# A DLRM tower on one core: the group loop written out, ten tables looked up by matmul, ids in small loads

## The reference

```python
e = jnp.stack([tbl_f[ids[:, f]] for f in range(27)], axis=1)      # 2048 x 27 x 128
z = jnp.einsum('bfd,bgd->bfg', e, e)[:, tril_i, tril_j]           # 2048 x 351
h = jnp.concatenate([z, dense_ctx], axis=1)                       # 2048 x 367
h = jnp.maximum(h @ W_top1 + b_top1, 0.0)                         # 512
h = jnp.maximum(h @ W_top2 + b_top2, 0.0)                         # 256
y = h @ W_top3                                                    # 1
```

## Time and profile before

| what | value |
| --- | --- |
| runs | 441.11, 441.77, 443.19 us |
| the profiled execution | 439.78 us, of it 437.9 us span |
| PE, matmul | 338.7 us busy, 77% |
| POOL | 297.9 us, 68% |
| DVE | 231.5 us, 53% |
| ACT | 212.2 us, 48% |
| mean granted clock of TensorE | 0.934 of full |
| bytes moved by DMA | 37.40 MB, mean 85 GB/s |
| table 0 landed, first lookup on PE | 19.92 us, 24.53 us |

### The profile page before, as it was taken

The page is one execution under the profiler, slowest core; times in us unless marked ns, Lnnn a source line. Parts: engine busy times, 40 slices in busy tenths (PEclk is TensorE's granted clock), DMA queues, the critical chain, the costliest instruction groups (busy, mean ns, idle before and its releaser), DMA issues.

```text
span 437.9 us, 14262 instructions
## 1 busy us (share of the span) xinstructions
PE 338.7 (77%) x5982; PEld 303.4 (69%) x5982; DVE 231.5 (53%) x907; ACT 212.2 (48%) x431; POOL 297.9 (68%) x308
## 2 busy tenths in 40 slices
PE   0071784798969898998843799799989789899778
PEld 0061683698859776987733798598869777897665
DVE  0290995497248623965431482487439544860430
ACT  1121746536573538434830136834584268436832
POOL 6777687777777777777777506777777777777020
PEclk9997798699998989999966599989999999999999
DMA  3748415265224522372227401236226922221000
GB/s 73 254 153 269 183 36 161 63 82 133 53 59 82 141 53 56 72 136 65 57 70 82 126 0 45 57 78 139 58 54 71 145 62 58 54 64 52 8 9 4
DMA packets 23740, 37.40 MB, mean 85 GB/s; under 512 B 6616, under 2 KB 17440, under 8 KB 23680
## 3 DMA queue, kind: packets, MB, share of 16 engines
q0 software_dynamic: 9600, 19.33, 15.7%
q10 hardware_dynamic: 10416, 10.75, 15.6%
q1 hardware_dynamic: 3664, 6.43, 4.2%
HBM read 35.61 MB, written 0.01 MB: 81 GB/s over the span
## 4 chain that ended last, share of the span: by engine, by line
PE 48%; SPq 12%; ACT 12%; DMA 11%; issue 11%; DVE 4%; ACTq 0%; DVEq 0%
SPq L280 12%; PE fill_ps L431 11%; PE fill_ps L433 10%; ACT et L544 9%; PE pair_ps L492 9%; PE mlp_ps L443 9%; PE mlp_ps L469 7%; DMA hot_ids<-ids_hot_d 4%; DMA work<-tbl_d 4%; DMA work<-dense_d 2%; DVE work L329 2%; DMA work<-work 1%; ACT work L329 1%; PE fill_ps L457 1%; DVE one_hot L638 1%
## 5 line engine op out<-in xcount | busy, mean ns | idle before, releaser
L394 POOL DMA_INDIRECT rows<-tbl_d,index x222 | 215.9, 973 | 82.3 <-issue 67.0
L431 PE MATMUL fill_ps<-one_hot,table_hi 128*128 128x256 f32 x610 | 159.6, 299 | 54.0 <-DVE table_lo L616 24.5
L431 PEld LDWEIGHTS fill_ps<-one_hot,table_hi 128*128 128x128 f32 x610 | 125.4, 206 | 56.4 <-issue 43.3
L433 PE MATMUL fill_ps<-one_hot,table_lo 128*128 128x256 f32 x610 | 157.1, 295 | 0.0
L638 DVE TENSOR_SCALAR one_hot<-hot_ids 128x256 fp32r<-128x256 f32 x610 | 137.3, 301 | 26.2 <-PE fill_ps L433 25.3
L329 DVE COPY work<-pair_ps 26x112 f32<-26x112 f32 (+1 forms) x256 | 66.0, 258 | 117.8 <-PE pair_ps L492 114.7
L433 PEld LDWEIGHTS fill_ps<-one_hot,table_lo 128*128 128x128 f32 x610 | 125.5, 206 | 0.0
L394 POOL DMA_INDIRECT rows<-tbl_d,ids_sb x72 | 78.1, 1084 | 26.4 <-issue 21.3
L552 ACT COPY et<-fill_ps 128x512 f32<-128x512 f32 (+1 forms) x37 | 42.5, 1148 | 106.5 <-PE fill_ps L433 102.6
L544 ACT COPY et<-fill_ps 128x512 f32<-128x512 f32 (+2 forms) x80 | 78.9, 1183 | 3.0 <-PE fill_ps L417 2.9
L492 PE MATMUL pair_ps<-et 128*26 128x26 f32 x4096 | 55.3, 196 | 29.9 <-issue 16.1
(11 more groups left out here) (24 smaller groups left out, 63.3 us busy)
## 6 DMA issues: line engine op xcount, KB each, us to landing
hot_ids<-ids_hot_d ACTq DMA_DIRECT2D x8, 1152.0 KB
rows<-tbl_d,index POOLq DMA_INDIRECT x222
work<-tbl_d SPq DMA_DIRECT2D x4, 512.0 KB, 18.5
work<-tbl_d SPq DMA_DIRECT2D x3, 640.0 KB, 16.4
rows<-tbl_d,ids_sb POOLq DMA_INDIRECT x72
w_sb<-w_d ACTq DMA_DIRECT2D x1, 768.0 KB, 4.8
w_sb<-tbl_d SPq DMA_DIRECT2D x1, 640.0 KB, 17.3
w_sb<-tbl_d SPq DMA_DIRECT2D x1, 512.0 KB, 17.9
```

The lines of the kernel that those rows point to most:

```text
L394: nc.gpsimd.indirect_dma_start(out=rows[:, t, c, :], out_offset=None, in_=tables[f], in_offset=bass.IndirectOffsetOnAxis(ap=numbers[:, f:f ...
L431: nc.tensor.matmul(to, table_hi[0:HOT_ROWS, CHUNK_AT[k] + c, :], hot, start=(c == 0), stop=False)
L433: last = nc.tensor.matmul(to, table_lo[0:HOT_ROWS, CHUNK_AT[k] + c, :], hot, start=False, stop=(c == HOT_CHUNKS[k] - 1))
```

## The change

The loop is gone; all groups are written out, and all engines walk one list of steps. In it the last two pair banks of a group stand between the lookups of the next one, and layer 2 is cut in two, so that no two pair banks touch but the last two. All groups use ten hot tables (90 chunks) and 17 cold ones. The hot ids come two tables at a time (256 KB), six loads ahead: the first six from ACT's queue, the others from SP's. They are no longer made local: DVE compares the raw int32 ids with a scalar per partition (`chunk_row`, the number of the row that the partition holds in this chunk). The one-hots lie in a ring of 20 chunks and are handed over by half tables. POOL and PE wait for each fill of up to four tables instead of each tile. ACT moves hot fills 0 and 1 only after it has moved bank 3 of the group before, since `et` is read until then. At the start, the long load of the other ids stands behind the first three tables.

```diff
-N_HOT = 9
-EARLY_HOT = (9, 9)
-LATE_HOT = (8, 9)
-HOT_RING = 3
+N_HOT = [10] * 8
+FILL_RING = 4
+IDS_RING = 6
+ONE_HOT_RING = 20
...
+def hot_fills(g):
+    return [(k, min(2, N_HOT[g] - k)) for k in range(0, N_HOT[g], 2)]
+def cold_fills(g):
+    n = FEATURES - N_HOT[g]
+    return [(c, min(4, n - c)) for c in range(0, n, 4)]
+def order():
+    steps = []
+    for g in range(GROUPS):
+        hot = [("hot", g, j) for j in range(len(hot_fills(g)))]
+        cold = [[("cold", g, t, j) for j in range(len(cold_fills(g)))] for t in range(GROUP_TILES)]
+        if g == 0:
+            steps += hot[:3] + cold[0] + hot[3:] + [("pairs", g, 0)] + cold[1][:2] + [("pairs", g, 1)] + cold[1][2:]
+        else:
+            b = g - 1
+            steps += [hot[0], ("pairs", b, 2), hot[1], ("pairs", b, 3), hot[2]] + cold[0][:2] + [hot[3]] + cold[0][2:4]
+            steps += hot[4:] + cold[0][4:] + [("layer1", b), ("pairs", g, 0)] + cold[1][:2]
+            steps += [("layer2", b, 0), ("pairs", g, 1)] + cold[1][2:] + [("layer2", b, 1), ("layer3", b)]
+    return steps + [("pairs", GROUPS - 1, 2), ("pairs", GROUPS - 1, 3)]
+STEPS = order()
...
+def halves(k):
+    n = CHUNKS_OF[k]
+    return (0, n // 2), (n // 2, n)
+def parts_in_the_way(end):
+    return sum(1 for last in ([0] + PART_ENDS)[:-1] if last < end - ONE_HOT_RING)
...
-        index = sb("index", [P, 2, GROUP_TILES * FEATURES], I32)
-        hot_ids = sb("hot_ids", [P, 2, N_HOT, COLS], I32)
-        one_hot = sb("one_hot", [P, HOT_RING, MAX_CHUNKS, COLS], F32R)
+        hot_ids = sb("hot_ids", [P, IDS_RING, 2 * COLS], I32)
+        one_hot = sb("one_hot", [P, ONE_HOT_RING, COLS], F32R)
...
-        def periods(engine, period, peeled=1):
-            period(0, 0)
-            period(0, 1)
-            with engine.Fori(1, GROUPS // 2 - peeled) as turn:
-                period(turn, 0)
-                period(turn, 1)
...
+        def load_hot_ids(engine, step):
+            _, g, j = step
+            k0, n = hot_fills(g)[j]
+            slot = HOT_FILL[step] % IDS_RING
+            engine.dma_start(hot_ids[:, slot, 0:n * COLS],
+                             ids_hot[g, k0 * COLS:(k0 + n) * COLS].partition_broadcast(P)
+                             ).then_inc(hot_ids_in[slot], 16)
...
         @block.sync
+            sp.dma_start(ids_sb[:, 0:FEATURES], ids[:, 0:FEATURES]).then_inc(first_ids_in, 16)
+            for k in range(3):
+                load_table(k)
+            sp.dma_start(ids_sb[:, FEATURES:], ids[:, FEATURES:]).then_inc(ids_in, 16)
+            for k in range(3, MOST_HOT):
+                load_table(k)
+            fills = list(HOT_FILL)
+            for step in STEPS:
+                if step[0] == "hot" and HOT_FILL[step] + IDS_RING < len(fills):
+                    sp.wait_ge(hot_made, parts_through(step))
+                    load_hot_ids(sp, fills[HOT_FILL[step] + IDS_RING])
+                elif step[0] == "pairs" and step[2] == PAIR_BANKS - 1 and step[1] < LAST:
+                    complete_zt(sp, step[1], ALL_LOWS, z_in)
+                elif step[0] == "layer3":
+                    store(step[1])
...
         @block.gpsimd
+                    for j, (c0, n) in enumerate(cold_fills(g)):
+                        if g > 0:
+                            freed = ("cold", g - 1, t, min(j, len(cold_fills(g - 1)) - 1))
+                            pool.wait_ge(cold_full, COLD_FILL[freed] + 1)
+                        for c in range(c0, c0 + n):
+                            f = COLD[c]
+                            nc.gpsimd.indirect_dma_start(
+                                out=rows[:, t, c, :], out_offset=None, in_=tables[f],
+                                in_offset=bass.IndirectOffsetOnAxis(
+                                    ap=ids_sb[:, tile * FEATURES + f:tile * FEATURES + f + 1].bitcast(U32), axis=0),
+                            ).then_inc(rows_in[t][j], 16)
...
         @block.tensor
+                    for half, (c0, c1) in enumerate(halves(k)):
+                        part, first = PARTS[step, k, half]
+                        pe.wait_ge(hot_made, part + 1)
+                        for c in range(c0, c1):
+                            hot = one_hot[:, (first + c - c0) % ONE_HOT_RING, :]
+                            nc.tensor.matmul(to, table_hi[:, CHUNK_AT[k] + c, :], hot, start=(c == 0), stop=False)
+                            last = nc.tensor.matmul(to, table_lo[:, CHUNK_AT[k] + c, :], hot,
+                                                    start=False, stop=(c == CHUNKS_OF[k] - 1))
+                        last.then_inc(hot_used, 1)
...
         @block.scalar
+            for step in list(HOT_FILL)[:IDS_RING]:
+                load_hot_ids(act, step)
...
+            for step in STEPS:
+                if step[0] == "hot":
+                    if step[1] == 0:
+                        for k in range(2 * step[2] + 4, min(2 * step[2] + 6, MOST_HOT)):
+                            make_high(k)
+                    if step[1] > 0 and step[2] < 2:
+                        early.append(step)
+                        continue
+                    move_hot(step)
+                elif step[0] == "cold":
+                    move_cold(step)
+                elif step[0] == "pairs":
+                    pairs(step)
+                    if step[2] == PAIR_BANKS - 1:
+                        for filled in early:
+                            move_hot(filled)
+                        early = []
+                elif step[0] == "layer2":
+                    relu2(step[1], step[2])
...
         @block.vector
-                    nc.vector.tensor_scalar(ids.bitcast(F32), ids, first_row[0:HOT_ROWS, n:n + 1], None, ALU.subtract
-                                            ).then_inc(hot_ids_local, 1)
...
+            def make_one_hots(step, k):
+                for half, (c0, c1) in enumerate(halves(k)):
+                    part, first = PARTS[step, k, half]
+                    wait_count(dve, hot_used, parts_in_the_way(first + c1 - c0))
+                    for c in range(c0, c1):
+                        last = nc.vector.tensor_scalar(one_hot[:, (first + c - c0) % ONE_HOT_RING, :],
+                                                       hot_ids[:, slot, (k - k0) * COLS:(k - k0 + 1) * COLS],
+                                                       chunk_row[:, at + c:at + c + 1], None, ALU.is_equal)
+                    last.then_inc(hot_made, 1)
...
+            for step in STEPS:
+                if step[0] == "hot" and NEXT_HOT.get(step, ("hot", 0, 0))[1] > 0:
+                    following = NEXT_HOT[step]
+                    for k in tables_of(following):
+                        make_one_hots(following, k)
+                elif step[0] == "pairs":
+                    _, g, bank = step
+                    if bank == 0:
+                        wait_count(dve, z_in, g * (16 * MOVES))
+                    move_pairs(dve, g, bank, (0, 1), pair_moved_v, nc.vector.tensor_copy)
+                elif step[0] == "layer3":
+                    output(step[1])
```

More of the change, by code:

```diff
@@ L276, in complete_zt @@
                 if low == 0:
[L277 removed]
+                    engine.dma_start(zt[row:row + DENSE, chunk, :],
+                                     dense[:, g * COLS:(g + 1) * COLS]).then_inc(dense_in, 16)
                 else:
@@ L420, in look_up, with transposes @@
-            def look_up(turn, h, n0, j):
-                k0, n = HOT_FILLS[j]
-                bank = fill_bank(turn, h, n0)
+            def transposes(step):
+                _, g, t, j = step
+                c0, n = cold_fills(g)[j]
+                pe.wait_ge(rows_in[t][j], gathered(g, t, j))
+                bank = fill_bank(step)
+                for c in range(n):
+                    last = nc.tensor.transpose(bank[:, c * P:(c + 1) * P], rows[:, t, c0 + c, :], ident[:, :])
+                last.then_inc(cold_full, 1)
@@ new lines, in row_pairs @@
+            def row_pairs(step):
+                _, g, bank = step
+                t = bank // TILE_BANKS
+                if bank % TILE_BANKS == 0:
+                    pe.wait_ge(fill_moved, 1 + max(FILL["cold", g, t, len(cold_fills(g)) - 1],
+                                                   FILL["hot", g, len(hot_fills(g)) - 1]))
+                wait_count(pe, pair_moved_v, BANK[step] - 1)
+                wait_count(pe, pair_moved_a, BANK[step] - 1)
+                for r in range(BANK_ROWS):
+                    for s in range(STRIPS):
+                        row = t * P + s * STRIP + bank % TILE_BANKS * BANK_ROWS + r
+                        last = nc.tensor.matmul(
+                            pair_ps[bank % 2][32 * s:32 * s + PAIR_COLS, r * PAIR_COLS:(r + 1) * PAIR_COLS],
+                            et[:, row, 0:FEATURES - 1], et[:, row, 1:FEATURES], start=True, stop=True)
+                last.then_inc(pair_full, 1)
@@ L597, in _, with relu1, relu2 @@
-            for k in range(3):
-                make_high(k)
```

(12 more changed lines are left out.)

477 lines of the change are left out of this document (177 added, 300 removed).

## The result

The changed kernel takes 419.12 us (median of four runs, 418.8 to 421.49) where the kernel before takes 442.48 (median of four, 441.11 to 445.17): a ratio of 0.9484, 95% interval 0.9429 to 0.9538. 414 was forecast. The profiled execution has a span of 419.6 us, against 437.9 before; it took 421.49 us, the longest of the four, where the others had spans of 416.9 to 417.5.

The account below looks back on a forecast made before the run. The prediction saw PE's work with small waits, POOL's gathers and SP's queue setting the pace. Start 63 + 7 x 46.2 + 5 + 19 = 410.4 us of span, 414 at the median's level; range 394 to 432.

Parts of the forecast that it names:

- Start: Up to the first lookup of group 1: 63 us instead of 83.8, with table 0 landing at 18.
- Period: One group on PE: 42.4 us of work, 1.95 and 0.9 of waits, 1.0 for hand-overs, 46.2 us in all.
- I take the first, as input and scalar are the same: DVE's new one-hot priced like the localising form, 267 ns for 256 columns, not like the subtraction with two tensor inputs.
- Rival 2: DVE's one-hots at the two-input price: 2 to 3.5 us more a group, 11 at the start, about 445; 3%.
- Layer 3 waits for ACT: PE waits 1.95 us a group for relu2, which stands behind bank moves and cold copies in ACT's program.
- Layer 1 waits for zt: PE waits 0.9 us a group: rows land 17.1 us after the bank, PE has 16.2 of work; bounds 0 and 8.
- Rival 1: SP's 14 moves still issue slowly: layer 1 waits 7 us more in seven groups, 463 us; 8%.
- POOL: 34 gathers at 1.285 us are 43.7 us a group, so POOL no longer sets the pace.
- rival 3: POOL's gathers set the pace, 425 us at the median, or the start gains nothing, 423; together 15%.
- Rival 4: Lean: neither the layer 3 nor the layer 1 wait appears and POOL's 43.7 us is the period, 397 us; 19%.
- Rival 5: DVE's one-hots and POOL's gathers exclude each other at the shared port: 61.7 us a group, over 520; 1%.
- Tail: After the periods: two touching banks with one issue wait, 5 us, then 19 us to the end.

Follow-up runs that it names:

- e2_ids_pieces_b: Kernel before, loop written out, each 1152 KB ids load cut into five contiguous pieces: 419.91 us against 442.76; without _b, 724.62 against 737.1.
- e3_local_b: Changed kernel with ids made local again and one-hots compared with an immediate: median 408.44 us against 442.76, 407.11 for the three of four runs that lie together.
- e7_local_layer2: Changed kernel with ids made local, one-hots against an immediate, and layer 2's second half ahead of the last transposes: 392.56 us against 441.12.
- e1_no_loop_b: Kernel before with its loop written out, nothing else: 435.36 us against 441.12, ratio 0.9849; without _b, 726.44 against 737.1.
- e10_local_nine: Changed kernel with ids made local, one-hots against an immediate, and nine hot tables instead of ten: 604.48 us against 729.06, ratio 0.8275.

## Why the prediction was right, and which of its terms were not

The forecast's sum was 63 + 7 x 46.2 + 24 = 410.4 us of span; measured are 61.9 + 334.1 + 23.6 = 419.6. The kind of result and the range were right: 414 us forecast, 419.12 measured, 23 us gained of the 28 forecast. The mechanism of a period was not. One of the prediction's own signs of being wrong was "one-hots are over 0.3 us apart", and they are 0.31 apart. That the number held all the same is partly luck, since this loss met errors of the other sign.

*Start.* Forecast 63, measured 61.90, by luck (and the terms given for the 63 add up to 61.8). Table 0 was forecast to land at 18, between 12 and 22, and was there at 7.03: I took the old landing for a matter of bytes in flight, and it was almost all the form of the ids load: with the pieces alone, and the order of the loads as it was, e2_ids_pieces_b has table 0 at 8.45. (Its first lookup comes only at 17.1 us, 24.5 before and 10.9 after, since DVE waits there until 12.1 for all five pieces.) Against these 11 us stood DVE's time for ten tables, 32.5 us forecast, 40.7 measured, from the dearer one-hots, and 2.7 us more between DVE's last one-hot of group 0 and group 1. Table 4 landed 7.2 us after its issue, about 5 forecast.

*Period.* Forecast 46.2, measured 47.7. The step that failed is the price of the new one-hot, "I take the first, as input and scalar are the same". It took two means of the localising form, 907 and 747 ns, drew their slope of 160 ns per 256 columns, and went down three steps to 267. e3_local_b gives that form at 256 columns as 375 ns: a slope wrong by some tens of nanoseconds, used three times. And it priced the form by its duration, which shows only 60 of the 100 ns that the distance between starts grew by. Rival 2 named the true place and nearly the true size (0.33 us apart; measured 0.31), though not the cause, which is the scalar and not a second tensor. It forecast 2 to 3.5 us a group and 11 in the start; e3_local_b gives 1.8 a group, and DVE's time in the start grew by 8. Its 445 did not come about, since table 0 was there 11 us before the forecast and 5 before its lower bound, and both losses were smaller. By its mechanism rival 2 occurred, and I had given it 3%. The sum has no term for the clock either: in the changed kernel the first lookups of a group take 5.5 us instead of 4.0 in four of the seven groups.

*Layer 3 waits for ACT.* Forecast 1.95 us, measured 1.70 to 1.97 in each of seven groups. e7_local_layer2 takes it away, and 1.9 us a period with it. This is the step that was best worked out, and the wait was an avoidable cost of the new order.

*Layer 1 waits for zt.* Forecast 0.9, measured none; the moves took 10.3 to 10.8 us against 10.98 forecast. Rival 1, moves of 18 us, fell. The reason given, that SP's program keeps the loads apart, is not what e2_ids_pieces_b shows: there loads and moves are in flight together, and the moves are quick.

*Back edge.* The hole is gone, as forecast. Its price was not worked out apart in the forecast; e1_no_loop_b shows 6 us, as POOL's waits for PE and a later start of group 1 come in its place.

*POOL.* "34 gathers at 1.285 are 43.7 us a group" held: it is the period of e7_local_layer2, 44.0. In the changed kernel POOL was not the pace, so rival 3 fell. The sign "POOL waiting for PE" is weak, 5.2 us in all; the 57 us behind its last gather show it better. Rival 4, the lean case, forecast 397 with neither wait and POOL as the pace; that is near the kernel e7_local_layer2, 392.56. Rival 5, exclusion by the port, fell: a gather takes 998 ns in the mean beside the longer one-hots.

*Tail.* 24 forecast, 23.6 measured, with 2.06 us of issue wait in the last two banks.

Where the 5% comes from, then: loop 6 us, small contiguous ids 15 more (to 419.9), and there POOL binds. The tenth table (272 gathers instead of 294, some 29 us less at 1.30) and the new order lift that bound, which is worked out and not measured by a run of its own. The per-partition scalar (14.4 us of span, 419.6 to 405.2) and relu2 behind the copies (14.1, 405.2 to 391.1) take back all that this could give; by the medians, 419.12, 407.11 and 392.56, they are 12 and 14.5. The order of the two undone edits matters: the second was measured with the first in place.

## What to carry to other kernels

Compare the distance between two producer instructions with the time that the consumer needs for one unit: here the consumer needs 0.24 us, so at 0.21 the producer costs nothing in a long run and at 0.31 it is the pace. Read the price of a form at the size at which it is used, and as a distance between starts; don't extrapolate from means at four times the size. Count a hole that is removed only up to the bound that stands next behind it; and when a load is slow, look at its packets before its bytes.

## What the runs showed of the hardware that I had not expected

- One broadcast load in rows of 1 KB slows other queues far more than five contiguous ones of the same bytes: with 10416 packets in place of 6832, at the same 10.75 MB, SP's 14 moves take 17.9 us and not 10.3, and a table lands in 19.3 and not 7.6.
- A DVE tensor_scalar of 128x256 starts 0.33 us after the one before it with a per-partition scalar and 0.22 us with an immediate, in runs of eight (0.31 and 0.21 in the long runs); int32 instead of fp32 as input costs nothing.
- The same kernel takes 1.65 to 1.67 times as long on some chips (729 to 737 us against 441 to 442), where PE waits for "issue" between small matmuls; why is open. There everything in the change but the loop, the pieces of ids and the tenth table, the order above all as I read it, is worth some 16% (ratios 0.8275 for e10_local_nine, 0.9838 for e2_ids_pieces and 0.9882 for e1_no_loop).
- After the wait of 1.7 us before layer 3 at 205.30, the next lookups start 0.12 us apart up to 206.77, then 0.21 us apart (0.41 us each, granted 1.2 GHz instead of 2.4) until 209.97. Without that wait (e7_local_layer2) the first run of lookups of a group takes 4.0 to 4.1 us in all seven groups; with it, 5.5 us in four groups of the changed kernel, and 4.0 in two others behind the same wait. So the wait goes with a fall of the clock, but not each time.
